# Group tables first, two recurrences summed on TensorE, the gate in the denominator, corrections in opposite row halves, and new orders

## The chip, the cores and the metric

The kernel runs on one core of a Trainium2 chip. The metric is the device time of one execution in microseconds (us). TensorE is called PE in the profile, its weight loads PEld; VectorE is DVE, ScalarE is ACT, GpSimd is POOL, and SyncE (SP) only issues DMAs.

## The reference, cut to what matters

`x` and `f` are 4 batches of 256 tokens by 256 channels. A bidirectional recurrence is computed for every batch and used as a token mixer twice (layer 1 ahead of the attention with gate `r = x`, layer 2 ahead of the feed-forward part with the new `x`):

```python
nf, df = scan(ekv, ek)            # a = a*decay + ekv ; b = b*decay + ek, forward in time
nb, db = scan(ekv, ek, reverse)   # the same backward
num = nf + nb - ekv + euk*vf
den = df + db - ek + euk
out = sigmoid(r) * (num / maximum(den, 1e-8)) * (0.8 + 0.2*tf)
```

Then come 16 query heads over 4 key heads with normed queries and keys, causal softmax and `Wo`; `x` is added. Then a router takes the 8 best of 64 experts in 8 groups, with a softmax inside each group (`soft`), and a gated feed-forward of 8 groups of 176 columns follows:

```python
xg = x[:, None, :] + einsum('ngi,ghi->ngh', soft, mask_up_w)
g, u = xg @ gate_proj, xg @ up_proj      # per group
y = sum over groups of scalar * (silu(g) * u) @ down_proj
```

The kernel never forms `xg`. It multiplies `mask_up_w` with the gate and up tables once (the group tables), and adds `soft @ table` as one extra matmul, the correction, to `x @ gate_proj` and to `x @ up_proj`.

## The kernel before, in words

Everything stays in SBUF with channels or tokens on the 128 partitions. Products that need accuracy are made of three fp32r matmuls (high by high, high by low, low by high; the helper `three`); small ones are single fp32 matmuls, each of which is two instructions in the profile.

Each engine runs a written list of steps in order. `START` holds the first steps of each engine by hand. Then `make_plan` walks through places 0 to 38; in each place the engine's entry in `ORDERS` says in which order it takes the parts of 32 attention items (A is a query projection, B its transposes, C scores, X exp, S the softmax sums, D transposes of the probabilities, E values, F the `Wo` product of two items), the key and value steps (`kv`) and the background steps (`bg`: weight splits, recurrence calls, routing). After place 38 the feed-forward part runs over 22 tiles of 128 columns (11 for each half of the tokens): GA is the gate product of a tile, GB the up product, Y the down product of the tile two back.

Start. SP loads `fT`, the constants, `xT`, the key weights and the eight group tables (six into buffers that are free early, two through the staging buffers). DVE computes the recurrence of batch 0, `("wkv", 1, 0, k)`: k=2 the product (L878), k=3 and 4 the four scans (L868) and the bonus term (L888), k=5 and 6 the sums and the division by way of ACT's Ln and Exp (L893 to L917). Then ACT rounds the result to `RH` (L693), DVE forms the rest `RL` (L921), and PE begins with the key projection K1. The table products `("R", g)` (L1171, eight matmul instructions for each group in fp32) stand behind the first K1. Batch 1 follows on DVE in the same manner. Table results wait in the PSUM banks `acc` and are copied by ACT (L747) and DVE (L1038) into `EX`. The gate of layer 1 is ACT's tanh of `xT` (L666) and a multiply by `1 + tanh` on the numerator (L909).

Feed-forward. PE order is GA, GB, Y for every tile. GA and GB are six matmuls of 128x512 each (L1126 to L1128) and then the correction `EX` by `SX` over all 128 rows (L1303; two of them in tile 5 of each half, which touches both halves of the table). `SX` is made by two transposes in `route` (L1268), a copy (L804) and a DVE step (L1000). DVE then forms the product (L1099, L1103, L1108), ACT and POOL split it (L822, L616), and Y follows.

Of the kernel before, what the change touches and what calls it, by code (L numbers as in the profile page):

```python
# [17 lines left out]
E = G * GS  # L18
# [15 lines left out]
def table_col(g):  # L34

    return g * FI - SECOND * (g // 4)
EXP_CAP = math.exp(KCAP)

# [13 lines left out]
            ("rest", 0)],  # L52
    "DVE": [("kv", 0), ("kv", 0), ("bg", 0), ("kv", 0), ("bg", 0), ("A", 0), ("D1", 4),
            ("kv", 0), ("bg", 0), ("F", 6), ("N", 0), ("S", 2), ("rest", 0), ("kv", 0),
            ("L", 5), ("C", 1)],
    "POOL": [("bg", 0), ("S", 2), ("bg", 0), ("bg", 0), ("rest", 0)],
# [3 lines left out]
    "ACT": ["GT", "split", "last", "GH"],  # L60
# [17 lines left out]
def kv_k(p, half):  # L78
# [5 lines left out]
    "PE": [("split", "K", 0), ("small",), ("split", "Q", 0), ("K1", 0, 0), ("R", 0), ("K1", 0, 1), ("R", 1),  # L84
           ("R", 2), ("R", 3), ("R", 4), ("R", 5), ("K3", 0, 0), ("K3", 0, 1)],
    "ACT": [("wkv", 1, 0, 1), ("tanh", 0), ("tanh", 1), ("tanh", 2), ("tanh", 3), ("logs",), ("wkv", 1, 0, 6),
            ("split", "K", 0), ("wkv", 1, 0, 7), ("small",), ("wkv", 1, 1, 1), ("split", "Q", 0), ("K1", 0, 0), ("K1", 0, 1),
            ("K2", 0, 0), ("wkv", 1, 1, 6), ("K3", 0, 0), ("K3", 0, 1)],
    "DVE": [("wkv", 1, 0, 0), ("wkv", 1, 0, 2), ("wkv", 1, 0, 3), ("wkv", 1, 0, 4), ("wkv", 1, 0, 5), ("wkv", 1, 0, 6), ("wkv", 1, 0, 8),
            ("wkv", 1, 1, 0), ("split", "K", 0), ("wkv", 1, 1, 2), ("wkv", 1, 1, 3), ("wkv", 1, 1, 4), ("K1", 0, 0), ("K1", 0, 1),  # L90
            ("wkv", 1, 1, 5), ("K2", 0, 0), ("wkv", 1, 1, 6)],
    "POOL": [("split", "K", 0), ("small",)],
# [3 lines left out]
    "PE": {"R": None, "split": None, "small": None, "K1": None, "V": None, "K3": None, "GA": None, "GB": None,  # L96
           "route": (0, 1, 3, 4, 6, 7, 8)},
    "ACT": {"split": None, "small": None, "K1": None, "V": None, "K2": None, "K3": None, "table": None,
            "wkv": (1, 6, 7), "gate": (0, 1), "route": (0, 2, 3, 5, 6, 7, 8)},
    "DVE": {"K1": None, "K2": None, "table": None, "onehot": None, "wkv": (0, 2, 3, 4, 5, 6, 8), "gate": (0, 1),  # L100
            "route": (1, 2, 4, 5, 6, 7)},
    "POOL": {"split": None, "small": None, "zeros": None},
# [13 lines left out]
def make_plan(engine, order, ffn_order):  # L116
# [7 lines left out]

    for i, st in ((2, ("split", "V", 0)), (0, ("R", 6)), (0, ("R", 7)), (0, ("table", 0)), (3, ("table", 1)),
                  (2, ("onehot",)), (15, ("zeros",)),
                  (10, ("split", "K", 1)), (17, ("split", "V", 1))):
        put(bg, i, st)
    calls = {(1, 1): [0, 0, 0, 0, 0, 0, 0, 0, 0], (1, 2): [3, 4, 4, 4, 4, 6, 6, 7, 7], (1, 3): [7, 8, 8, 8, 10, 11, 12, 12, 12],
             (2, 0): [12, 13, 13, 14, 14, 15, 16], (2, 1): [18, 19, 19, 19, 20, 21, 21],  # L130
             (2, 2): [21, 21, 22, 22, 23, 24, 24], (2, 3): [25, 26, 26, 26, 26, 28, 28]}
# [7 lines left out]
    for n, back in enumerate([-2, -2, -2, -1, -3, -2, -2, -3]):  # L139
        put(bg, max(first_tile(*divmod(n, NKV)) + back, 0), ("split", "Q", n))  # L140
    for n, on in enumerate([5, 5, 5, 5, 3, 5, 5, 4]):
        put(bg, first_tile(*divmod(n, NKV)) + on, ("split", "O", n))
    early = [31, 35, 37]
# [3 lines left out]
    for half, places in (((0, 1), [2, 4, 4, 5, 5]), ((1, 0), [15, 15, 15, 16, 17]), ((1, 1), [17, 18, 18, 19, 19])):  # L147
        for i, st in zip(places, kv_k(*half)):
            put(kv, i, st)
    for p, places in ((0, [3, 5, 6, 6]), (1, [21, 21, 23, 24])):  # L150
        for t, i in enumerate(places):
            put(kv, i, ("V", p, t))
    ahead = []
    for f, places in enumerate(([36, 37, 37], [45, 45, 45])):
# [39 lines left out]
    for st, f in zip(last, [0, 1, 2, 3, 4, 5, 6, 6, 8, 9, 10]):  # L194
        if concerns(engine, st):
            per[f].append(st)
# [23 lines left out]
BLOCKS = [s for s in PLAN if s[0] in ("small", "split") or s[0] == "R" and s[1] >= 6]  # L220
# [3 lines left out]
BLOCK_COLS = {"R": 4 * FI, "small": 256, "K": 1024, "V": 1024, "Q": 1024, "O": 1024, "F": 768}  # L224
# [39 lines left out]
ND = {1: 17, 2: 16}  # L264
NA = {1: 5, 2: 4}


def wkv_before(count, layer, b):

    return sum(count[call[0]] for call in WKV_CALLS[:WKV_CALL[(layer, b)]])  # L270


def last_call(layer, b):
    return wkv_before(ND, layer, b) + ND[layer]
# [40 lines left out]

def spread_count(f):
# [4 lines left out]
def program(nc, ins, out, group_scalars):  # L321
    ctx = ExitStack()
    with ctx:
# [21 lines left out]
        half = sb("half", [P, B])  # L345
        half_mix = sb("half_mix", [P, B])
        edec = sb("edec", [P, 8])
# [9 lines left out]
        E2, F2, B2 = (sb(n, [P, 2 * CH * TE]) for n in ("E2", "F2", "B2"))  # L357
# [11 lines left out]
        V = sb("V", [P, TPP, NKV * D])  # L369
# [15 lines left out]
        bmask = V[:, :, :].rearrange("p t n -> p (t n)").rearrange("p (c g d e) -> p c g d e", c=CH, g=G, d=16)  # L385
        mup = sb("mup", [P, CH, E])

        def early_table(g):

            if g < 4:  # L390
# [24 lines left out]

        acc = [pb("acc0"), pb("acc1")]
# [6 lines left out]
        names = """consts_in vecs_in cond_in side_in0 side_in1 side_in2 side_in3 x_in0 x_in1 x_in2 x_in3 table_in0 table_in1 table_in2 table_in3 table_in4 table_in5 mup_in imap_in stores_done  # L423
        pads_ready half_ready init_act init_dve zeros_ready key_scale_ready bmask_ready onehot_ready scalars_out
        split_hi split_lo ffn_used
        wkv_act wkv_dve tanh1_done r1_ready r2_ready tanh2_done base_gated rh2_done
# [56 lines left out]
        def _(sp):  # L483
            def load(n):
                step = BLOCKS[n]
                if n >= NSTAGE:
                    old = BLOCKS[n - NSTAGE]
                    if old[0] == "R":
                        sp.wait_ge(s["table_full"], RNO[old] + 1)
                    else:  # L490
                        sp.wait_ge(s["split_lo"], SPLIT_NO[old] + 1)
                w = BLOCK_COLS[step[1] if step[0] == "split" else step[0]]
                if step[0] == "R":
                    src = ins["tables"][step[1]]
                elif step[0] == "small":
# [17 lines left out]
            side(0)  # L513
            sp.dma_start(const[:], ins["const"]).then_inc(s["consts_in"], 16)
            main(0)
            sp.dma_start(mup[:], ins["mup"]).then_inc(s["mup_in"], 16)
            main(1)
            main(2)
            main(3)
            load(0)  # L520
            side(1)
            table(0)
            table(1)
            table(2)
            load(1)
            table(3)
            load(2)
            table(4)
            table(5)
# [5 lines left out]
            def spread_scalars(f):  # L535
                p, m = divmod(f, FT)
                if m == 0:
                    tok = slice(p * PT_, (p + 1) * PT_)
                    sp.wait_ge(s["rt_act"], 7 * p + 7)
# [22 lines left out]
        def _(pool):  # L562
# [7 lines left out]
            linked(pool.memset(V[:], 0.0))  # L570
# [3 lines left out]
            pool.wait_ge(s["mup_in"], 16)  # L574
            for g in range(G):
# [796 lines left out]
```

## Time and profile before

| | before |
|---|---|
| median of 3 runs | 420.47 us (418.64 to 420.99) |
| the profiled execution: its time / its span | 419.07 us / 417.3 us |
| PE busy | 367.4 us (88%) |
| DVE busy | 331.4 us (79%) |
| ACT busy | 275.9 us (66%) |
| POOL busy | 218.5 us (52%) |
| chain that ended last | PE 53%, DVE 25%, ACT 15%, issue 5% |

The span goes from the first to the last instruction; the time of the execution has 1.8 us more around it. Busy shares are means over the span: PE does next to nothing in the first 20 us and is never idle in the feed-forward part, so the table is to be read together with the rows by stretch.

### The profile page before, as it was taken

Reading aid. Unit: us, or ns where it says so; the run is one execution under the profiler, and the core shown is the slowest. Engines: PE = TensorE matmul, PEld = TensorE weight load, DVE = VectorE, ACT = ScalarE, POOL = GpSimd, SP = SyncE. Lnnn points to the kernel's source line nnn. Section 1 sums busy time; section 2 is a strip of 40 time slices with the busy share of each in tenths; the row PEclk is TensorE's granted clock in tenths of the full one; section 3 lists DMA queues with packets and bytes.
Section 4 is the critical chain, followed back from the end, with each engine's and each line's share of the span. In section 5 each row is a group of like instructions: output and inputs, shape, how many; then the busy total and the mean of one; then the engine's idle time right before and its main releaser. Section 6 shows DMA issues by size and latency. Waiting matters only on the chain.

```text
span 417.3 us, 6425 instructions
## 1 busy us (share of the span) xinstructions
PE 367.4 (88%) x1952; PEld 294.3 (71%) x1952; DVE 331.4 (79%) x779; ACT 275.9 (66%) x673; POOL 218.5 (52%) x229
## 2 busy tenths in 40 slices
PE   0098778899999789898998987999899999999995
PEld 0097566688878667687776876687587878888884
DVE  8999788999988997789999889486557777665543
ACT  5547778798889498696976887785375434453321
POOL 7160613179524858225585121464259756888831
PEclk9999989999999999999999999999999999999999
DMA  7735300113100304001031000111065343274121
GB/s 214 297 87 183 104 0 0 52 52 102 53 0 2 102 0 137 15 3 50 2 101 40 1 2 0 38 41 38 2 160 172 138 126 81 97 218 173 53 75 50
DMA packets 14209, 31.92 MB, mean 76 GB/s; under 512 B 1872, under 2 KB 4432, under 8 KB 14176
## 3 DMA queue, kind: packets, MB, share of 16 engines
q1 hardware_dynamic: 13888, 31.38, 23.6%
q8 instruction: 16, 0.26, 0.3%
q10 hardware_dynamic: 288, 0.14, 0.1%
q14 instruction: 17, 0.14, 0.1%
HBM read 30.43 MB, written 1.08 MB: 76 GB/s over the span
## 4 chain that ended last, share of the span: by engine, by line
PE 53%; DVE 25%; ACT 15%; issue 5%; POOLq 0%; POOL 0%; DVEq 0%; ACTq 0%
PE ov L1223 6%; PE sc L1201 5%; PE acc L1126 4%; PE acc L1127 4%; PE acc L1128 4%; PE tr L1152 4%; ACT PR L623 4%; DVE B L868 3%; DVE F L868 3%; DVE PR L1062 3%; PE proj L1140 3%; PE tr L1128 2%; PE tr L1126 2%; PE tr L1127 2%; PE sc L1126 2%
## 5 line engine op out<-in xcount | busy, mean ns | idle before, releaser
L596 POOL TENSOR_TENSOR WL<-stage,WH 128x256 fp32r<-128x256 f32 x142 | 125.9, 916 | 75.1 <-ACT WH L662 75.1
L610 POOL TENSOR_TENSOR PR<-PR,RI 128x512 f32<-128x512 f32 x48 | 53.6, 1133 | 83.8 <-DVE RI L1072 83.8
L1140 PE MATMUL proj<-WH,RH 128*128 128x512 f32 x96 | 42.5, 443 | 33.0 <-DVE RL L921 19.9
L1126 PE MATMUL acc<-OH,WH 128*128 128x256 f32 (+1 forms) x172 | 54.5, 317 | 2.9 <-DVE OL L1084 2.2
L623 ACT ACTIVATE PR<-PR,MX 128x128 f32<-128x128 f32 (+1 forms) x128 | 56.9, 458 | 0.0
L1127 PE MATMUL acc<-OL,WH 128*128 128x256 f32 (+1 forms) x172 | 53.1, 309 | 0.0
L1128 PE MATMUL acc<-OH,WL 128*128 128x256 f32 (+1 forms) x172 | 53.0, 308 | 0.0
L1201 PEld LDWEIGHTS sc<-kT,QT 128*128 128x128 f32 x256 | 41.6, 193 | 16.1 <-issue 12.9
L1201 PE MATMUL sc<-kT,QT 128*128 128x128 f32 (+1 forms) x256 | 47.8, 330 | 0.0
L1223 PE MATMUL ov<-PTS,V 128*128 128x512 f32 x96 | 46.6, 594 | 1.1 <-DVE OL L1084 1.1
L1140 PEld LDWEIGHTS proj<-WH,RH 128*128 128x128 f32 x96 | 18.4, 192 | 39.5 <-issue 37.2
L1062 DVE CUSTOM_DVE_ANT_0 PR<-sc,const,RQ 128x128 f32<-128x128 f32 (+1 forms) x128 | 45.5, 412 | 0.1
L822 ACT CAST OH<-PR 128x512 fp32r<-128x512 f32 x22 | 13.7, 623 | 42.2 <-DVE PR L1108 42.1
L616 POOL TENSOR_TENSOR OL<-PR,OH 128x512 fp32r<-128x512 f32 x22 | 28.9, 1312 | 22.5 <-ACT OH L822 21.0
L662 ACT CAST WH<-stage 128x768 fp32r<-128x768 f32 (+1 forms) x42 | 39.3, 937 | 0.0
L1141 PE MATMUL proj<-WH,RL 128*128 128x512 f32 x96 | 38.7, 403 | 0.0
L1126 PEld LDWEIGHTS acc<-OH,WH 128*128 128x128 f32 x172 | 32.4, 188 | 6.0 <-issue 2.8
L1099 DVE SCALAR_TENSOR_TENSOR PR<-PR,sc 128x512 f32<-128x512 f32 x22 | 15.1, 686 | 25.1 <-ACT PR L814 25.1
L1128 PEld LDWEIGHTS acc<-OH,WL 128*128 128x128 f32 x172 | 32.4, 188 | 2.0
L1127 PEld LDWEIGHTS acc<-OL,WH 128*128 128x128 f32 x172 | 32.4, 188 | 2.0
L927 DVE TENSOR_REDUCE SS<-SQ 128x4 f32<-128x512 f32 x40 | 26.8, 677 | 5.5 <-ACT SQ L719 5.5
L1144 PE MATMUL proj<-WL,RH 128*128 128x512 f32 x96 | 30.8, 402 | 0.0
(160 smaller groups left out, 878.4 us busy)
## 6 DMA issues: line engine op xcount, KB each, us to landing
stage<-in_ffn SPq DMA_DIRECT2D x22, 384.0 KB, 3.3
stage<-in_wq SPq DMA_DIRECT2D x8, 512.0 KB, 3.3
stage<-in_wo SPq DMA_DIRECT2D x8, 512.0 KB, 3.4
SBC<-group_scalars SPq DMA_DIRECT2D x8, 256.0 KB, 3.6
PR<-in_tables SPq DMA_DIRECT2D x4, 352.0 KB, 7.2
fT<-in_fT SPq DMA_DIRECT2D x4, 256.0 KB, 3.8
xT<-in_xT SPq DMA_DIRECT2D x4, 256.0 KB, 4.1
stage<-in_wk SPq DMA_DIRECT2D x2, 512.0 KB, 4.7
```

The lines of the kernel that those rows point to most:

```text
L596: i = pool.tensor_tensor(lo[:, c:c + 256], src[:, c:c + 256], hi[:, c:c + 256].bitcast(F32), ALU.subtract)
L610: pool.tensor_tensor(pr, pr, RI[:, m % 4, hs[0]:hs[0] + nh].rearrange("p (h o) -> p h o", o=1).broadcast_to([P, nh, 512 // nh]), ALU.mult) ...
L623: return nc.scalar.activation(o, i, ACT.Exp, **k)
L662: nc.scalar.copy(WH[:, slot, 0:w], src[:, 0:w]).then_inc(s["split_hi"], 1)
L1062: i = v.tensor_tensor_reduce(PR[:, u % 6, w * k:w * k + w], sc[u % 2][:, w * k:w * k + w], mask[:, 256 - w:256], RQ[:, n % NST, half_, h:h ...
L1126: mm(o, lh, rh, start=first, stop=False, skip_group_check=True)
L1127: mm(o, lh, rl, start=False, stop=False, skip_group_check=True)
L1128: return mm(o, ll, rh, start=False, stop=last, skip_group_check=True)
L1140: mm(proj[:], rh[ch], wh[ch], start=ch == 0, stop=False, skip_group_check=True)
L1141: mm(proj[:], rl[ch], wh[ch], start=False, stop=False, skip_group_check=True)
L1201: i = mm(sc[u % 2][:, w * k:w * k + w], QT[:, m % 3, h, :], kT[:, g, T * bb:T * bb + w], start=True, stop=True)
L1223: i = mm(ov[:], V[:, 2 * bb + c, g * D:(g + 1) * D], PTS[:, m % 2, c, :, :].rearrange("p h n -> p (h n)"), start=(c == 0), stop=(c == ti))
```

## The change

1. **Tables.** All eight table products stand in PE's `START` list, R0 to R6 ahead of the first key projection and R7 right behind it, and all eight tables are loaded early, each into a free buffer. SP's order is new: `fT` of batch 0, `mup`, table 0, the constants, `xT` of batch 0, tables 1 and 2, the key weights, tables 3 and 4, `fT` of batch 1, tables 5 to 7, the router's weights, `xT` of batch 1, the query weights, and only then `xT` of batches 2 and 3. POOL lays out the masked table of `mup` with one copy in place of eight. The rows of the up table are rotated by 64 against those of the gate table (`table_rows`), so each copy of a group is made in two pieces of 176 columns in place of one of 352.
2. **Sums.** For batches 0 and 1 of layer 1 PE adds the forward recurrence, the backward one and the bonus term by identity matmuls in fp32 into PSUM (three for the denominator, three for the numerator). DVE reads the sums there.
3. **Gate.** ACT makes `exp(-x)` in place of tanh, POOL clamps it and adds 1, and DVE multiplies it into the denominator in the step that takes the maximum (all four batches of layer 1). The multiply on the numerator is gone.
4. **Projections** issue the two matmuls that need only `RH` before they wait for `RL`.
5. **Corrections.** A tile's correction reads only the 64 rows of its pair of groups: for the gate product in one row half, for the up product in the other. From tile 2 on, both are issued one after the other ahead of GA's six matmuls, into two PSUM banks. Tiles 2 and 8 of each half still use all 128 rows; tile 5 has the pair and one full correction for each product. Tiles 0 and 1 issue a 64-row correction at the end of GA and of GB. The up corrections need `SX` with its row halves exchanged (`SY`), which two DMAs on SP's queue make for each half of the tokens.
6. **Orders.** `ORDERS`, the places of many background steps and GB of tile 0 are changed.

```diff
     "PE": [("R", 0), ("R", 1), ("R", 2), ("sum", 0, 0), ("R", 3), ("sum", 0, 1), ("sum", 0, 2),
            ("R", 4), ("R", 5), ("R", 6), ("K1", 0, 0), ("R", 7), ("split", "K", 0), ("small",),
            ("split", "Q", 0), ("K1", 0, 1), ("sum", 1, 0), ("sum", 1, 1), ("K3", 0, 0), ("K3", 0, 1), ("sum", 1, 2)],
     "ACT": [("ex", 0), ("wkv", 1, 0, 1), ("wkv", 1, 0, 6), ("ex", 1), ("split", "K", 0), ("wkv", 1, 0, 7), ("small",), ...
...
-    "PE": [("kv", 0), ("kv", 0), ("kv", 0), ("kv", 0), ("kv", 0), ("D0", 4), ("bg", 0),
-           ("A", 0), ("kv", 0), ("D1", 4), ("kv", 0), ("F", 6), ("E", 5), ("bg", 0),
-           ("kv", 0), ("C", 1), ("B", 0), ("rest", 0)],
+    "PE": [("kv", 0), ("kv", 0), ("kv", 0), ("kv", 0), ("bg", 0), ("D0", 4), ("A", 0),
+           ("kv", 0), ("D1", 4), ("kv", 0), ("F", 6), ("E", 5), ("bg", 0), ("kv", 0),
+           ("C", 1), ("B", 0), ("kv", 0), ("bg", 0), ("rest", 0)],
...
+                elif st[0] == "sum":
+                    _, b, k = st
+                    n0 = wkv_before(ND, 1, b)
+                    for x, n, kind in ((DF, 3, 0), (DB, 4, 0), (EUX[:], 5, 0), (NF, 6, 1), (NB, 7, 1), (EU[:], 9, 2)):
+                        if kind == k:
+                            pe.wait_ge(s["wkv_dve"], n0 + n)
+                            i = mm(sum_bank(b, min(k, 1)), ident, x, start=n in (3, 6), stop=n in (5, 9), skip_group_check=True)
...
                 elif k == 5:
+                    if summed(L, b):
+                        dve.wait_ge(s["sum_ready"], 2 * b + 1)
+                        dve.wait_ge(s["gate_ready"], b + 1)
+                        done(v.scalar_tensor_tensor(out=DF, in0=sum_bank(b, 0), scalar=1e-8, in1=gate1(b), op0=ALU.max, op1=ALU.mult))
+                        return
...
+                elif st[0] == "ex":
+                    b = st[1]
+                    act.wait_ge(s[f"x_in{b}"], 16)
+                    exp(gate1(b), xT[:, :, cols(b)], scale=-1.0).then_inc(s["gate_exp"], 1)
...
+                    def both(h, row, first, last):
+                        i = correct(0, h, slice(row, row + 64), first, last)
+                        correct(1, h, slice(64 - row, 128 - row), first, False)
+                        return i
...
+                    side_by_side = f >= 2 and pairs
+                    if side_by_side and a == 0:
+                        wait_bank(1)
+                        wait_soft(1)
+                        both(*pairs[0], True, False)
...
+                    for r in (0, 64):
+                        sp.dma_start(turned_soft(p)[64 - r:128 - r, :, :].bitcast(F32), SX[r:r + 64, :, tok].bitcast(F32)).then_inc(s["soft_turned"], 16)
```

## Rows read from the trace of the kernel before

**Rows 1.** The page, busy time of the engines over the span.
```profile
PE 367.4 (88%) x1952; PEld 294.3 (71%) x1952; DVE 331.4 (79%) x779; ACT 275.9 (66%) x673; POOL 218.5 (52%) x229
```
**Rows 2.** Busy time by stretch: stretch, length, busy of each engine, clock, DMA share, GB/s.
```profile
21.00:45.00 24.00, 20.99 (x117) 18.62 (x115) 22.89 (x39) 15.04 (x32) 10.44 (x9) 1.00 0.39 119
45.00:80.00 35.00, 28.65 (x137) 22.18 (x138) 29.04 (x85) 27.68 (x76) 11.75 (x14) 0.95 0.14 45
200.00:300.00 100.00, 92.11 (x538) 72.31 (x537) 82.61 (x239) 74.15 (x199) 43.91 (x46) 1.00 0.09 27
340.00:360.00 20.00, 20.00 (x95) 16.07 (x94) 16.25 (x23) 9.24 (x16) 14.58 (x16) 1.00 0.29 82
```
**Rows 3.** Waits of PE: for whom, us in total, times, longest.
```profile
PE proj L1140 <- DVE RL L921: 19.9, 1, 19.9
```
**Rows 4.** Timeline of batch 0: start, length, engine, line, operation.
```profile
9.69 1.20 DVE L868 TENSOR_TENSOR_SCAN B<-DEC,E 128x514 f32<-128x514 f32 x1
13.67 0.43 DVE L899 TENSOR_SCALAR F<-F 128x512 f32<-128x512 f32 x1
17.59 0.75 DVE L917 SCALAR_TENSOR_TENSOR F<-F,half_mix 128x512 f32<-128x512 f32 x1
18.38 0.62 ACT L693 CAST RH<-F 128x512 fp32r<-128x512 f32 x1 [2.02 <-DVE F L917]
```
**Rows 5.** Timeline of batch 1 on DVE.
```profile
30.78 0.69 DVE L895 TENSOR_TENSOR EU<-EUX,fT 128x512 f32<-128x512 f32 x1
31.39 0.69 DVE L897 TENSOR_TENSOR F<-F,EUX 128x512 f32<-128x512 f32 x1
37.83 0.75 DVE L917 SCALAR_TENSOR_TENSOR F<-F,half_mix 128x512 f32<-128x512 f32 x1
38.50 2.35 DVE L1038 SCALAR_TENSOR_TENSOR EX<-EX,const,acc 32x352 fp32r<-32x352 f32 x4
```
**Rows 6.** Timeline of PE: two matmuls of the first projection, then table products.
```profile
20.43 0.63 PE L1141 MATMUL proj<-WH,RL 128*128 128x512 f32 x1
20.86 0.63 PE L1140 MATMUL proj<-WH,RH 128*128 128x512 f32 x1
22.57 2.29 PE L1171 MATMUL acc<-PR,V 128*128 128x176 f32 x8
29.66 2.55 PE L1171 MATMUL acc<-PTS,V 128*128 128x176 f32 x16
```
**Rows 7.** The chain that ended last: two fp32 value matmuls of 512 columns.
```profile
79.19 1.72 PE ov L1223 x4
```
**Rows 8.** Timeline: POOL's mask copies in the first 12 us.
```profile
6.02 5.70 POOL L576 COPY V<-mup 128x48 f32<-128x48 f32 x8 [2.00 <-DMA mup<-in_mup]
```
**Rows 9.** The page's DMA issues: count, KB of each, median us from issue to landing.
```profile
SBC<-group_scalars SPq DMA_DIRECT2D x8, 256.0 KB, 3.6
```
**Rows 10.** The page, DMA traffic in 40 slices of 10.4 us.
```profile
GB/s 214 297 87 183 104 0 0 52 52 102 53 0 2 102 0 137 15 3 50 2 101 40 1 2 0 38 41 38 2 160 172 138 126 81 97 218 173 53 75 50
```
**Rows 11.** Timeline of PE around four 64-row transposes inside the feed-forward part.
```profile
321.63 0.40 PE L1128 MATMUL acc<-OH,WL 128*128 128x512 f32 x1
321.95 0.32 PEld L1255 LDWEIGHTS proj<-const,LT 64*128 64x128 f32 x4 [0.37 <-issue]
321.96 0.46 PE L1255 MATMUL proj<-const,LT 64*128 64x64 f32 x4
322.35 0.19 PEld L1126 LDWEIGHTS sc<-RH,WH 128*128 128x128 f32 x1
...
322.69 0.39 PE L1127 MATMUL sc<-RL,WH 128*128 128x512 f32 x1
...
322.92 0.40 PE L1128 MATMUL sc<-RH,WL 128*128 128x512 f32 x1
```
**Rows 12.** Timeline: `SX` of the first half complete, and GB's first correction.
```profile
301.30 0.75 DVE L1000 SCALAR_TENSOR_TENSOR SX<-SX,const,proj 128x512 fp32r<-128x512 f32 x1 [1.97 <-ACT SX L804]
...
306.98 0.39 PE L1303 MATMUL tr<-SX,EX 128*128 128x512 f32 x1
```

More of the change, by code:

```diff
@@ L59 @@
     "PE": ["GA", "GB", "Y", "last", "split"],
-    "ACT": ["GT", "split", "last", "GH"],
+    "ACT": ["GT", "last", "split", "GH"],
     "DVE": ["GU", "last", "out"],
@@ L83 @@
 START = {
[L84 to L92, printed above, removed]
[3 rows of a table added]
+    "ACT": [("ex", 0), ("wkv", 1, 0, 1), ("wkv", 1, 0, 6), ("ex", 1), ("split", "K", 0), ("wkv", 1, 0, 7), ("small",),
+            ("wkv", 1, 1, 1), ("split", "Q", 0), ("K1", 0, 0), ("K1", 0, 1), ("K2", 0, 0), ("wkv", 1, 1, 6), ("K3", 0, 0),
+            ("K3", 0, 1)],
@@ L101 @@
             "route": (1, 2, 4, 5, 6, 7)},
-    "POOL": {"split": None, "small": None, "zeros": None},
+    "POOL": {"ex": None, "split": None, "small": None, "zeros": None},
 }
@@ L218 @@
 PLAN = PLANS["PE"]
-BLOCKS = [s for s in PLAN if s[0] in ("small", "split") or s[0] == "R" and s[1] >= 6]
+BLOCKS = [s for s in PLAN if s[0] in ("small", "split")]
 BLOCK_NO = {s: n for n, s in enumerate(BLOCKS)}
@@ L313, in group_rows, with table_rows, packed @@
     return [(g, max(g * FI - P * m, 0), min((g + 1) * FI - P * m, P)) for g in range(first, last + 1)]
+def table_rows(g, a):
+    first = 32 * ((g + 2 * a) % 4)
+    return slice(first, first + 32)
+def packed(m):
+    pairs = sorted({g // 2 for g, _, _ in group_rows(m)})
+    return [] if len(pairs) == 2 and pairs[0] // 2 == pairs[1] // 2 else [(q // 2, 64 * (q % 2)) for q in pairs]
 def spread_count(f):
@@ L513, in _ @@
             side(0)
+            sp.dma_start(mup[:], ins["mup"]).then_inc(s["mup_in"], 16)
+            table(0)
             sp.dma_start(const[:], ins["const"]).then_inc(s["consts_in"], 16)
             main(0)
-            sp.dma_start(mup[:], ins["mup"]).then_inc(s["mup_in"], 16)
+            table(1)
+            table(2)
+            load(0)
+            table(3)
+            table(4)
+            side(1)
+            table(5)
+            table(6)
+            table(7)
+            load(1)
             main(1)
+            load(2)
             main(2)
             main(3)
[L520 to L529, printed above, removed]
             sp.dma_start(imap[:], ins["imap"]).then_inc(s["imap_in"], 16)
@@ L1296, in _ @@
                     for ch in range(CH):
                         w = wblock(wst, 256 * a + P * ch, 256 * a + P * ch + P)
-                        three(bank[:], w[0], w[1], RH[:, p, ch, :], RL[:, p, ch, :], ch == 0, False)
-                    pe.wait_ge(s["rt_vec"], 6 * p + 6)
-                    if f == 0:
-                        pe.wait_ge(s["table_lo"], 2)
-                    for h, c0 in halves:
-                        i = mm(bank[:], EX[:, h, a, c0:c0 + P], SX[:, h, tok], start=False, stop=(h, c0) == halves[-1], skip_group_check=True)
+                        i = three(banks[a][:], w[0], w[1], RH[:, p, ch, :], RL[:, p, ch, :], ch == 0 and not side_by_side,
+                                  bool(side_by_side) and ch == CH - 1 and len(pairs) == 1)
@@ new lines, in _ @@
+                    if side_by_side and len(pairs) == 2:
+                        i = correct(a, pairs[1][0], slice(0, P), False, True)
+                    if not side_by_side:
+                        wait_soft(a)
+                        if pairs:
+                            h, row = pairs[0]
+                            row = 64 - row if a else row
+                            i = correct(a, h, slice(row, row + 64), False, True)
+                        else:
+                            i = correct(a, group_rows(m)[0][0] // 4, slice(0, P), False, True)
```

241 lines of the change are left out of this document (146 added, 95 removed), and 9 rows, old and new, of tables (ORDERS, START).

## The prediction, as put on record

> **What bounds the kernel now.** I read the busy shares first [rows 1]: PE is busy for 367.4 of 417.3 us, DVE for 331.4, so neither alone explains the span. The busy time by stretch [rows 2] says where each counts. From 340 to 360 us, as in the whole feed-forward part from about 303 on, PE is busy 20.00 of 20.00 us: whatever PE does more or less there moves the end one for one. From 21 to 45 DVE is busy 22.89 of 24.00 and PE 20.99, but much of that PE work is table products that nobody waits for. From 45 to 80 PE idles 6.4 us, from 200 to 300 7.9 us. Then the waits of PE: one of 19.9 us [rows 3], for the first projected batch. So there are three parts: a start that runs at DVE's pace, a middle in which PE is the bound with small holes, and an end that is PE alone.
>
> **The start, batch 0.** Before, its scans end at 9.69 + 1.20 = 10.89, its result (L917) at 18.34 and the rounded copy at 19.00 [rows 4]. After, the bonus step moves between the scans, so the four scans end at about 11.5. PE must first do R0 to R2, then three fp32 identity matmuls. R0 waits for the mask: POOL's eight copies take 5.70 us [rows 8]; one copy of the same 384 columns is shown nowhere, between 0.7 (one of eight) and 5.7; I take 1.1, and `mup` is issued two DMAs sooner, so R0 starts near 6.3. A group costs 2.29 us at the slow matmul pace and half of 2.55, 1.27, at the fast one [rows 6]; that these are the two levels 1.2 and 2.4 GHz is read from the pace, 0.43 us from one 512-column matmul to the next at 20.43 and 20.86 [rows 6] against 0.23 later [rows 11]. PE began at 19.9, its table products from 22.57 still run at the slow pace, and everything from 24.6 on is fast. If it rises as soon after R0, R0 is slow, R1 mixed, R2 fast: 6.3 + 2.3 + 2.1 + 1.3 = 12.0. An fp32 matmul of 512 columns costs 1.72 / 2 = 0.86 us at the fast level [rows 7], three 2.6: the denominator stands at 14.6, about 0.5 later than the 14.10 at which the maximum step ends now [rows 4]. The numerator's three (2.6) and R3 (1.3) follow, until 18.5, and DVE's last step ends at 19.3 where it ended at 18.34.
>
> Between this and the key projection stands one new wait. ACT's `exp` for batch 1 is queued ahead of the key weights' cast and of batch 0's rounded copy, and waits for `xT` of batch 1, which SP now issues sixteenth. By the sizes listed 4.98 MB come before its end. The first two slices moved 2.23 and 3.10 MB [rows 10], which puts it at 10.4 + 2.75/0.297 = 19.7; with the tables, whose packets are larger, moved into the first slice, it can be 16.5. I take 18: exp to 18.6, cast to 19.65, copy to 20.3. DVE leaves batch 0 about 1.0 us later than now. K1 then finds PE free only after R4 to R6 (3.8 us), near 22.3, and ends near 23.7 at the fast pace, where it ends at 22.8 now; DVE reads it much later, so this is hidden behind the scans of batch 1.
>
> **Batch 1.** Between its scans and its result DVE loses two sums of the denominator, two of the numerator and the gate multiply, at 0.61 us apart (30.78 to 31.39, [rows 5]) 3.05 us, and gets 0.2 back, since the maximum step of 0.43 [rows 4] becomes one of 0.69: 2.85 saved. PE's six identity matmuls for it, 5.2 us, fall between 24 and 36, where 6.2 us and more of table products are gone: no cost. Result of batch 1: 38.58 now [rows 5], less 2.85, plus 1.0. The copies of tables in two pieces: DVE's four take 2.35 us [rows 5]; eight of half the columns cost between the same and double, I take +0.5. Start in sum: +1.0 - 2.85 + 0.5 = **-1.4** (bounds -3.5 and +2.5).
>
> **The middle.** Batches 2 and 3 lose the gate multiply and keep the adds: 2 x (0.61 - 0.2) = -0.8, worth that much where DVE leads. The granted clock was 0.95 of full from 45 to 80 [rows 2], after holes in PE's work: 5% of 35, 1.7 us, is lost to the 1.2 GHz level; if PE gets its first items earlier and with fewer holes, part comes back: -1.0 (bounds 0 and -1.7). The new orders cannot be priced from rows: they can at best close the holes of rows 2, of which I count less than half (-6), and can open new ones (+4); I take **-1.5**. The early matmuls on `RH` alone save nothing in the middle, where `RL` is long ready. Middle: **-3.3**.
>
> **The feed-forward part, where I look hardest.** Now a correction is one 128-row matmul at 0.23 us (322.69 to 322.92, [rows 11]); a pair 0.46. Of 22 tiles, tiles 2 and 8 of each half stay as they are and tiles 0 and 1 of the first half are single: 16 pairs. The trace has no 64-row pair, but it has 64-row matmuls amid 128-row ones. The last 128-row one starts at 321.63 and would give way at 321.86. The 64-row weights are not loaded ahead, as all others are: the load starts at 321.95. The next 128-row load starts at 322.35, also not ahead, and its matmul streams from 322.69 - 0.23 = 322.46, which prices a bare load at 0.11. In all 0.60 us for four loads that take 0.32 together: at least **0.28 us of switching** per visit [rows 11]. The other three visits of this kind look the same. A pair then costs 0.28 + load 0.11 + second load under the first matmul 0.11 + one stream 0.21 = 0.71, 0.25 more than now: 16 x 0.25 = 4.0. The four single ones cost 0.28 + 0.11 + 0.21 = 0.60 against 0.23: 4 x 0.37 = 1.5. Sum **+5.5**; bounds: if the two halves don't overlap, 16 x 0.11 more, +7.3; if nothing is switched, -3.7. I take +5.5, since it is the nearest row.
>
> The Trainium skill, TensorEngine Tiling (Array Packing), Key Properties, says that changing the tiling mode drains the array, though tiles within a mode work in parallel. The trace agrees with the drain, 0.09 us before the load and the missing prefetch; by its promise of up to 2x alone, the term would be -3.7.
>
> Waits added there: GB of tile 0 needs `SX` turned. `SX` is whole at 302.05 [rows 12], two issues on SP and a landing of 3.6 us (the scalars' loads of like size, [rows 9]) give 306.4, ahead of 306.98 where its first correction stands; behind PE is everything, so each us of lateness would count. GA of a tile now also waits for the up bank of the tile two back, free before in all but the routing stretches. SP's two DMAs a half lie ahead of the group scalars, for which DVE has waited already, and are hidden by PE's backlog. All at 0, bound +1.5.
>
> **Sum.** -1.4 - 3.3 + 5.5 = +0.8 on the profiled execution's 419.07 us (span 417.3 and 1.8 around it): 419.9. That execution lies 1.4 below the median of 420.47, by which it would be 421.3. I predict **420.5**.
>
> **Rivals.** (1) The likeliest, as above: start and middle give about what the end takes. Chance 0.50; own range 416.5 to 425.
>
> (2) The row halves work side by side with no switching cost. Each pair costs one matmul: -3.7 in place of +5.5, 9.2 less, 411 to 412. For it: fp32r streams of 512 columns appear nowhere in the visits I measured, those were fp32 of 64. Against it: all visits show the gap. Chance 0.30. The Trainium skill, TensorE: Matmul & The Clock Gate, Part 3, reports four 32-row tiles of 512 columns at 3.07 times; no row here shows one.
>
> (3) Slower: PE is not yet at 2.4 GHz when the sums come. R0 to R2 at 2.29 each from 6.3 reach 13.2, and three sums at the slow pace take 5.2, so the denominator comes at 18.4 in place of 14.6; DVE stands behind it, and all of batch 1. Start +3.8: 424.3. It decides from a rise later than about 12 us. Chance 0.12.
>
> (4) The orders open holes: the middle is +4 in place of -1.5, 426. Chance 0.08.
>
> A measurement of this kernel tells 0.5%, 2.1 us. Case 1 gives faster 0.10, same 0.22, slower 0.18; case 2 0.29 and 0.01; case 3 same 0.02, slower 0.10; case 4 same 0.02, slower 0.06. Faster 0.39, same 0.27, slower 0.34. Cases of both signs hold the chance, so the range reaches from case 2 to case 4: 411 to 427.
>
> **What would show it.** The first K1 matmul at 22 to 23; the result of batch 1 near 36.7; GA's pair at 0.7 us from the matmul before it to the first full one after (0.25 to 0.35 if I am wrong); the feed-forward part from its first GA to the end longer by 5 us. Denominator sums later than 16 us speak for case 3. The prediction fails above all if the 64-row visit is cheap for fp32r, or if the holes in the middle close by more than I count.

## The result, and the profile after

The changed kernel takes 428.50 us in the median (426.87 to 428.93, 4 runs) where the kernel before takes 419.62 (418.64 to 420.99, 4 runs): ratio 1.0208, 95% interval 1.0175 to 1.0240. It is 8.9 us slower, above my range of 411 to 427.

The page of the profiled execution (busy times, the clock by slices):

```profile
PE 386.0 (90%) x1976; PEld 297.6 (70%) x1976; DVE 331.8 (78%) x776; ACT 276.1 (65%) x680; POOL 216.3 (51%) x226
...
PEclk9998989899999999999999999999999999999999
```

The windows of [rows 2], with the same columns:

```profile
21.00:45.00 24.00, 20.09 (x84) 13.28 (x83) 21.77 (x33) 15.68 (x33) 9.07 (x9) 0.93 0.28 88
45.00:80.00 35.00, 25.74 (x124) 19.99 (x123) 28.89 (x91) 28.66 (x82) 13.93 (x15) 0.95 0.09 31
200.00:300.00 100.00, 94.83 (x567) 76.22 (x565) 85.58 (x246) 78.15 (x211) 40.41 (x43) 1.00 0.09 27
340.00:360.00 20.00, 20.00 (x93) 15.48 (x92) 16.65 (x25) 7.70 (x14) 14.60 (x16) 1.00 0.36 103
```

PE is busy 18.6 us longer in a span 9.3 us longer; part of it is new work, the twelve identity matmuls at 0.86 us each, and part is the same work at half the clock. From 45 to 80 it is busy for 25.74 us, with 9.3 us of holes where there were 6.4: what the reordering was hoped to close has opened. From 21 to 45 the granted clock is 0.93 where it was 1.00.

The start, by the timeline (compare [rows 4] and [rows 5]):

```profile
6.82 6.35 PE L1246 MATMUL acc<-PR,VX 128*128 128x176 f32 x24 [6.82 <-DMA const<-in_const]
10.32 1.23 DVE L921 TENSOR_TENSOR_SCAN F<-DEC,E 128x514 f32<-128x514 f32 x1
14.73 1.02 PE L1255 MATMUL sc<-EUX,const 128*128 128x512 f32 x2
15.79 0.69 DVE L965 SCALAR_TENSOR_TENSOR F<-sc,TH 128x512 f32<-128x512 f32 x1 [0.28 <-PE sc L1255]
19.56 0.76 DVE L938 SCALAR_TENSOR_TENSOR F<-ov,full_mix,F 128x512 f32<-128x512 f32 x1 [0.30 <-PE ov L1255]
20.35 0.62 ACT L742 CAST RH<-F 128x512 fp32r<-128x512 f32 x1 [0.90 <-DVE F L938]
22.82 0.75 PE L1218 MATMUL proj<-WH,RH 128*128 128x512 f32 x2
37.54 0.75 DVE L938 SCALAR_TENSOR_TENSOR F<-ov,full_mix,F 128x512 f32<-128x512 f32 x1 [0.74 <-PE ov L1255]
38.67 3.25 DVE L1115 SCALAR_TENSOR_TENSOR EX<-EX,const,acc 32x176 fp32r<-32x176 f32 x8 [0.38 <-ACT EX L799]
```

DVE waits twice for sums of PE. The result of batch 0 ends at 20.32 (18.34 before), that of batch 1 at 38.29 (38.58 before), and the copies of the first half of the table take DVE 3.25 us instead of 2.35. In between, the scans of batch 1 begin at 23.34 where they began at 21.71.

What follows on PE is the first query projection and the first scores. In the kernel before:

```profile
33.79 1.26 PE L1152 MATMUL tr<-const,RT 128*128 128x128 f32 x8 [1.58 <-DVE RT L1027]
34.89 1.36 PE L1171 MATMUL acc<-stage,V 128*128 128x176 f32 x8
...
37.01 0.62 PE L1144 MATMUL proj<-WL,RH 128*128 128x512 f32 x2
...
36.00:39.00 3.00, 3.00 (x20) 2.73 (x19) 2.93 (x5) 2.77 (x7) 0.00 (x0) 1.00 0.53 172
```

In the changed kernel:

```profile
34.33 1.26 PE L1232 MATMUL tr<-const,RT 128*128 128x128 f32 x8 [2.06 <-DVE RT L1103]
...
36.52 1.84 PE L1218 MATMUL proj<-WH,RH 128*128 128x512 f32 x2
38.16 1.05 PE L1221 MATMUL proj<-WH,RL 128*128 128x512 f32 x2
...
36.00:39.00 3.00, 3.00 (x6) 1.65 (x5) 1.85 (x4) 2.56 (x9) 0.00 (x0) 0.50 0.01 3
```

The table products that filled PE here are gone, it idles 2.06 us ahead of the key transposes (1.58 before), and from 36 to 39 us the granted clock is 0.50, the 1.2 GHz level. The first scores start at 42.39, where they started at 40.48: 1.9 us are lost before the second half of the table is copied.

Then the waits of PE from 40 to 100 us (total, times, longest):

```profile
PE proj L1218 <- ACT VX L791: 3.4, 3, 2.7
PE sc L1287 <- DVE MX L1139: 2.9, 1, 2.9
PE proj L1218 <- ACT SQ L768: 2.8, 2, 1.5
```

The middle one is new: scores wait for the maxima of the scores before them, which DVE has behind the copies of the second half of the table. The experiments turn on it. The first one has grown: its longest wait is 2.7 us, ahead of 80.06, where the kernel before has one of 1.0.

The feed-forward part, PE timeline around a pair of 64-row corrections (the column behind the tiles is rows by columns of the array in use):

```profile
354.35 0.60 PE L1356 MATMUL proj<-const,ST 128*128 128x128 f32 x4
354.88 0.49 PE L1392 MATMUL sc<-SX,EX 64*128 64x512 f32 x1
354.88 0.49 PE L1392 MATMUL tr<-SY,EX 64*128 64x512 f32 x1
355.30 0.50 PE L1203 MATMUL sc<-RH,WH 128*128 128x512 f32 x1
355.64 0.40 PE L1204 MATMUL sc<-RL,WH 128*128 128x512 f32 x1
```

The two start together. A 0.40 us record holds the 0.23 us from one full matmul to the next and 0.16 of pipeline, so the stream before ends at 354.79 and the first full stream behind begins at 355.64 - 0.23 = 355.41: the visit takes 0.62 us.

Milestones: PE's first `Wo` product starts at 91.2 us (85.1 before), its first product of the feed-forward part at 304.68 (300.34), its last at 422.57 (413.32). So 4.3 us have been lost by 304.7, and the feed-forward part is 117.9 long, not 113.0: 4.9 more. At 91 us 6.1 were lost; 1.8 of them are won back by 304.7.

### The profile page after: what moved, and what is told of

Read it like the earlier page. It is cut to its first block, busy times and chain, and to the rows that moved or that the text cites. A ratio compares the mean times of both kernels' runs of the same rounds, so it can differ in the third digit from the quotient of the medians.

```text
span 426.6 us, 6520 instructions
## 1 busy us (share of the span) xinstructions
PE 386.0 (90%) x1976; PEld 297.6 (70%) x1976; DVE 331.8 (78%) x776; ACT 276.1 (65%) x680; POOL 216.3 (51%) x226
## 4 chain that ended last, share of the span: by engine, by line
PE 56%; DVE 22%; ACT 14%; issue 5%; DMA 2%; SPq 1%; POOLq 0%; POOL 0%; ACTq 0%; DVEq 0%
PE ov L1311 6%; PE sc L1287 5%; PE tr L1232 5%; PE acc L1203 4%; PE acc L1205 4%; PE acc L1204 4%; DVE B L921 3%; DVE PR L1139 3%; PE sc L1203 3%; DVE F L921 3%; PE proj L1218 3%; ACT PR L674 2%; PE proj L1221 2%; PE tr L1203 2%; PE sc L1204 2%
## 5 line engine op out<-in xcount | busy, mean ns | idle before, releaser
L643 POOL TENSOR_TENSOR WL<-stage,WH 128x256 fp32r<-128x256 f32 x142 | 120.9, 880 | 94.2 <-ACT WH L713 94.2
L661 POOL TENSOR_TENSOR PR<-PR,RI 128x512 f32<-128x512 f32 x48 | 52.7, 1115 | 77.2 <-DVE RI L1149 77.2
L1311 PE MATMUL ov<-PTS,VX 128*128 128x512 f32 x96 | 46.6, 594 | 1.1 <-DVE OL L1161 1.1
L1218 PE MATMUL proj<-WH,RH 128*128 128x512 f32 x96 | 36.0, 457 | 11.9 <-ACT SQ L768 5.8
L667 POOL TENSOR_TENSOR OL<-PR,OH 128x512 fp32r<-128x512 f32 x22 | 29.2, 1328 | 14.6 <-ACT OH L874 13.5
L1232 PE MATMUL tr<-const,PR 128*128 128x128 f32 x192 | 29.2, 277 | 4.2 <-ACT QT L806 1.6
L1221 PE MATMUL proj<-WH,RL 128*128 128x512 f32 x96 | 30.9, 404 | 0.0
L1232 PEld LDWEIGHTS tr<-const,PR 128*128 128x128 f32 x192 | 22.8, 142 | 10.9 <-issue 6.4
```

What stands on the lines that cost most here:

```text
L643: i = pool.tensor_tensor(lo[:, c:c + 256], src[:, c:c + 256], hi[:, c:c + 256].bitcast(F32), ALU.subtract)
L661: pool.tensor_tensor(pr, pr, RI[:, m % 4, hs[0]:hs[0] + nh].rearrange("p (h o) -> p h o", o=1).broadcast_to([P, nh, 512 // nh]), ALU.mult) ...
L1218: mm(proj[:], rh[ch], wh[ch], start=ch == 0, stop=False, skip_group_check=True)
L1221: mm(proj[:], rl[ch], wh[ch], start=False, stop=False, skip_group_check=True)
L1232: i = tp(tr[t % 2][:, P * k:P * k + P], x, ident)
L1311: i = mm(ov[:], V[:, 2 * bb + c, g * D:(g + 1) * D], PTS[:, m % 2, c, :, :].rearrange("p h n -> p (h n)"), start=(c == 0), stop=(c == ti))
```

## The experiments

Ratios are to the kernel before, with 95% intervals; us that are worked out from ratios are shares of 419.6.

### 1. Key weights' exponential ahead of the first gate exponential

```diff
-    "ACT": [("ex", 0), ("wkv", 1, 0, 1), ("wkv", 1, 0, 6), ...
+    "ACT": [("wkv", 1, 0, 1), ("ex", 0), ("wkv", 1, 0, 6), ...
```

In the changed kernel ACT's list begins with a step that waits for `xT` of batch 0 until 8.34 us; the scans start at 10.32.

> ACT's first gate exponential, which waits for xT of batch 0 until 8.34 us, is issued behind the exponential of the keys instead of ahead of it. Theory A (that wait is what delays the start and all behind it): the scans of batch 0 begin near 6.5 us instead of 10.3, its result comes 2 to 4 us sooner than 20.3, and the kernel gets 3 to 4 us faster than the changed one (about 425). Theory B (PE's first three table groups, until 13.0 us, and the sums queued behind them set batch 0): the scans move but the denominator still leaves PE at 15.6, the result stays at 20.3 within 0.5 us, and the time stays at 428.5 within 1.

Measured 428.45 us, 1.0221 (1.0205 to 1.0237): nothing gained. The scans began at 7.81, 2.5 us sooner, and the step that makes the result of batch 0 began at 20.67, 1.1 us later than before the edit (19.56). DVE waited 3.40 us for PE's sum of the denominator: PE, with tables and sums, sets it.

### 2. Corrections and table layout as before

The changed kernel with whole 128-row corrections, no rotation, no `SY`, and table copies in one piece; starts, sums, gate and orders stay.

```diff
-    first = 32 * ((g + 2 * a) % 4)
+    first = 32 * (g % 4)
...
-                        both(*pairs[0], True, False)
...
+                    for h, c0 in halves:
+                        i = mm(bank[:], EX[:, h, a, c0:c0 + P], SX[:, h, tok],
```

> The corrections, the table copies and the row layout go back to those of the kernel before (all 128 rows, at the end of GA and GB, no exchanged halves, copies in one piece); all else is as changed. Theory A (the visits of PE to 64-row form cost what was forecast): the stretch from GB of tile 0 to the end shrinks by 4 to 5 us, and table copies give about 1 to 2 us more: 422 to 424. Theory B (the loss in the feed-forward part comes from the new waits and DMAs or from the orders): at most 1 to 2 us faster than the changed kernel.

Measured 421.17 us, 1.0051 (1.0035 to 1.0066). Of the 8.9 us this takes 6.6 back by the ratios, more than the corrections can owe; about half comes ahead of the feed-forward part (first `Wo` product at 88.0 us, not 91.2; first product of the feed-forward part at 301.44, not 304.68). The feed-forward part is 114.07 us long, still 1.1 more than in the kernel before. Runs 6, 9, 13, 14 and 15 follow the half ahead of it.

### 3. Both together

Edits 1 and 2.

> Both of the edits above. If they are independent, the gains add: 419 to 421 if the first exponential matters by itself, 422 to 424 if it does not.

Measured 420.46 us, 1.0033 (1.0021 to 1.0045): 0.8 us below run 2 by the ratios, the intervals overlap. It is the base of runs 7, 8, 11 and 12.

### 4. Each 64-row correction alone

```diff
-                    side_by_side = f >= 2 and pairs
+                    side_by_side = False
```

> The changed kernel with no two corrections side by side: each tile issues its 64-row correction at the end of GA and again at the end of GB, so 32 visits where there were 16. Theory A (the cost is one of each visit, near 0.4 us above a full correction): 16 x (2 x 0.61 - 0.62) = 9.6 us slower than the changed kernel, near 438. Theory B (the visit costs little, the wait ahead of GA costs): no slower, or faster by 1 to 2 us.

Measured 437.29 us, 1.0431 (1.0410 to 1.0452), 9.4 us above the changed kernel by the ratios. 32 visits in place of 16: what is paid is paid for each visit.

### 5. Both corrections in the same row half

```diff
-                        correct(1, h, slice(64 - row, 128 - row), first, False)
+                        correct(1, h, slice(row, row + 64), first, False)
```

> The changed kernel, but the up correction of each pair reads the same 64 rows as the gate correction, so the two cannot be in opposite halves (its values are then those of other groups; the number and form of the instructions are unchanged). Theory A (opposite halves do run at the same time): each of the 16 pairs grows from 0.62 to about 0.83 us, one stream of 0.21, so 3.4 us slower than the changed kernel, near 432. Theory B (they never overlapped, the pair's cost was two streams all along): no difference, 428.5.

Measured 431.57 us, 1.0294 (1.0263 to 1.0326), 3.6 us above. The timeline of PE around a pair:

```profile
354.50 0.60 PE L1356 MATMUL proj<-const,ST 128*128 128x128 f32 x4
355.03 0.49 PE L1392 MATMUL sc<-SX,EX 64*128 64x512 f32 x1
355.37 0.39 PE L1392 MATMUL tr<-SY,EX 64*128 64x512 f32 x1
355.68 0.50 PE L1203 MATMUL sc<-RH,WH 128*128 128x512 f32 x1
356.02 0.40 PE L1204 MATMUL sc<-RL,WH 128*128 128x512 f32 x1
```

The second starts 0.34 behind the first, not with it: opposite halves do run side by side, for about 0.22 us a pair (3.6 / 16).

### 6. Pieces without rotation

Run 2 with each group's copy in two pieces of 176 columns.

> The kernel with whole-row corrections (the run that took 421.17), but its table copies are made in two pieces of 176 columns on ACT and DVE, as in the changed kernel. Theory A (the pieces, which stand in front of the first scores on DVE, are what costs 3.3 us ahead of the feed-forward part): 3 us slower than that run, near 424. Theory B (the row layout or the mask costs): within 0.5 us of 421.2.

Measured 421.09 us, 1.0052 (1.0035 to 1.0069), as run 2. Pieces alone cost nothing here. The copies of one half of the table took 2.01 us on ACT and 2.88 on DVE, against 2.43 and 3.25 in the changed kernel, for as many pieces of the same size.

### 7. Only batch 1 summed on TensorE

```diff
-    return layer == 1 and b < SUMMED
+    return layer == 1 and b == 1
```

On run 3; batch 0 is added on DVE again.

> The kernel with whole-row corrections and the exponential of the keys first (420.46), but PE sums batch 1 only; batch 0 is summed on DVE as before. Theory A (PE's tables and sums are the gate of batch 0): its result comes near 18 us instead of 19.7 to 20.3, and the time falls by 1 to 2 us to about 419. Theory B (a lead of batch 0 is used up by batch 1's own order on DVE and PE): within 0.5 us of 420.5.

Measured 420.34 us, 1.0019 (1.0002 to 1.0036), no different from run 3. Batch 0 again ended at 20.2. DVE had met another hindrance near its start:

```profile
5.06 1.73 DVE L895 TENSOR_SCALAR half<-tf 128x4 f32<-128x4 f32 x1
```

The same step of 4 columns takes 0.17 us in run 11.

### 8. Orders of before on the new start

Run 3 with `ORDERS` and the places of the background steps as they were.

> The kernel with whole-row corrections and the exponential of the keys first (420.46), with the orders and places of the kernel before; the hand-written starts stay. Theory A (the new orders bring the 1.5 us that were forecast): 1 to 2 us slower, 421.5 to 422.5. Theory B (the new orders fit the old costs no better): the same within 0.5 us, or faster.

Measured 425.97 us, 1.0164 (1.0134 to 1.0193): 5.5 us slower than run 3. PE has no wait for the maxima from 40 to 100 us, as in the kernel before; other waits are longer, such as one of 2.3 us ahead of a query projection (1.3 in run 3).

### 9. Rotation without 64-row corrections

Run 6 with the up table's rows rotated and `SY` made, but all corrections over 128 rows.

```diff
-    first = 32 * (g % 4)
+    first = 32 * ((g + 2 * a) % 4)
...
+                        i = mm(bank[:], EX[:, h, a, c0:c0 + P], turned_soft(p)[:, h, :] if a else SX[:, h, tok],
```

> The kernel with whole-row corrections and table copies in pieces (421.09), plus the rotated rows of the up table and the two DMAs that exchange the halves of SX; the corrections still read all 128 rows at the end of GA and GB. Theory A (the rotated layout, whose copies change rows with every instruction, costs the 3 to 4 us that the changed kernel loses ahead of the feed-forward part): 424 to 425, with GB of tile 0 starting near 310. Theory B (that loss belongs to the 64-row form alone or is drift of the schedule): 421 within 0.7, at most 1 more for the DMAs.

Measured 425.58 us, 1.0150 (1.0129 to 1.0171): 4.1 us above run 6 by the ratios. Copies (2.43 and 3.25), the wait for the maxima (2.9) and the first `Wo` product (91.6) are as in the changed kernel.

### 10. The kernel before with the new orders

> The kernel before with only the new orders and places; its starts, sums, gate and corrections stay. Theory A (the new orders are better by themselves, as their 5.5 us in the run with the old orders suggest): 3 to 5 us faster than the kernel before, near 415. Theory B (orders fit only the costs that they were made for, so old with old and new with new): same as the kernel before or 1 to 4 us slower.

Measured 417.94 us, 0.9969 (0.9956 to 0.9981): 1.3 us faster than the kernel before, and the fastest kernel of the study. Its feed-forward part begins 2.3 us sooner (298.04) and is 1.1 us longer (114.10), so 1.1 us of what the new orders take from the middle comes back at the end. The wait for the maxima is there, too, with 1.10 us:

```profile
52.20 1.13 PE L1201 MATMUL sc<-kT,QT 128*128 128x128 f32 x8 [1.10 <-DVE MX L1062]
```

Against run 2, which has the same orders, the same corrections and the new start, sums and gate, it is 3.4 us faster by the ratios. Its first scores start at 40.49 (42.90 in run 2), and its clock from 21 to 45 us is 1.00 (0.93).

### 11. POOL clears the table ahead of the mask copy

Run 7, with POOL's clearing of `EX` moved ahead of its wait for `mup`.

> The kernel that sums batch 1 only on PE (420.34), with POOL's clearing of the table buffer ahead of the mask copy, as before. In that kernel DVE's small step beside the clearing took 1.73 us in place of 0.17 and the product 1.29 in place of 0.69. Theory A (POOL and DVE hold each other up there, and the start is DVE's): the scans begin near 6.4 in place of 7.8 and the time falls by 1 to 1.5 us. Theory B (absorbed at PE or later): within 0.4 us of 420.3.

Measured 420.06 us, 1.0017 (1.0001 to 1.0034), as run 7. DVE ended batch 0 at 18.5, 1.8 us sooner, but `RL` waited 1.39 us for ACT's `RH`, and the lead was gone.

### 12. No sums on TensorE

Run 7 without the sums of batch 1.

> The kernel that sums batch 1 only (420.34), with no sums on PE at all. Theory A (the sums of batch 1 shorten DVE's chain by 2.9 us at no cost, as forecast): 2 to 3 us slower, near 423. Theory B (PE's 5.2 us and the wait for its last sum eat the gain): within 0.7 us.

Measured 421.82 us, 1.0065 (1.0048 to 1.0082), 1.9 us above run 7 by the ratios: that is what the sums of batch 1 are worth. The result of batch 1 came at 40.13, 2.5 us later than in run 7 (37.58). PE, which had the sums to do in run 7, idled 9.1 us ahead of the key transposes and had a clock of 0.79 from 21 to 45 us (0.93), so part of the 1.9 can be the clock's.

### 13. Rotated, copies in an order that keeps the rows

```diff
-                    for g in range(4 * h, 4 * h + 4):
+                    for r in range(4):
                         for a in range(2):
+                            g = 4 * h + (r + 2 * a) % 4
                             rows = table_rows(g, a)
```

On run 9; the same eight pieces, and the two on the same rows follow each other.

> The rotated up table with whole-row corrections as in the run before it that measured 425.58 us, but the eight copies of a table half are ordered so that the two pieces that lie on the same 32 rows follow each other: the rows change four times in place of eight. Theory A (what the rotation costs comes from the change of rows between one small copy and the next, 46 to 50 ns each on ACT and DVE, 0.8 us for both engines and each half of the table): half of it goes, copies take 2.2 and 3.1 us in place of 2.43 and 3.25, and the time falls by at least 1.5 us, to 423 to 424. Theory B (the rotation costs in some other way, in the table products or by the exchanged copy of the softmax): the copies get shorter and the time stays at 425 to 426.

Measured 422.32 us, 1.0067 (1.0041 to 1.0093), 3.5 us below run 9 by the ratios. I had miscounted: rows change seven times in the old order and three times in the new one, which is the count of run 6, too. The copies take what they took there, 2.01 and 2.88. Each of four changes had cost 0.105 us on ACT (0.42 / 4) and 0.09 on DVE (0.37 / 4).

### 14. The same order in the changed kernel

> The changed kernel whole, with the copies of a table half in the same new order and nothing else. Theory A: 426 to 427 us, about 2 less than the 428.5 of the changed kernel. Theory B: 428 to 429.

Measured 425.77 us, 1.0140 (1.0115 to 1.0166): 2.9 us below the changed kernel by the ratios, with no instruction more or less.

### 15. Longer copies without rotation

Run 6 with every gate piece cut in two again, twelve copies in place of eight for each half of the table.

> No rotation, whole-row corrections, copies in pieces, as in the run that measured 421.09 us, but the gate piece of every group is cut in two once more: twelve copies for each half of the table in place of eight. By the step from four to eight (ACT 1.79 to 2.01 us, DVE 2.35 to 2.88) this adds 0.2 us on ACT and 0.5 on DVE for each half, together as much as the rotation added. Theory A (what counts is only how long ACT and DVE are held, whatever makes them longer): 423 to 425 us. Theory B (the rotation costs in another way than by the time of the copies): 421 to 421.5.

Measured 424.22 us, 1.0115 (1.0091 to 1.0138): 2.6 us above run 6, with 2.22 and 3.40 us of copies. The second scores and the windows from 45 to 60 us (PE busy, PEld, DVE, ACT, POOL, granted clock, DMA) show why so little weighs so much. Run 6:

```profile
54.08 1.13 PE L1283 MATMUL sc<-kT,QT 128*128 128x128 f32 x8 [1.75 <-DVE MX L1135]
...
45.00:60.00 15.00, 10.42 (x54) 8.07 (x53) 12.66 (x52) 12.74 (x43) 7.79 (x9) 1.00 0.20 70
```

Run 15:

```profile
55.82 2.05 PE L1283 MATMUL sc<-kT,QT 128*128 128x128 f32 x8 [2.72 <-DVE MX L1135]
...
45.00:60.00 15.00, 11.02 (x49) 9.09 (x48) 12.88 (x53) 11.52 (x42) 8.23 (x11) 0.89 0.20 70
```

The changed kernel:

```profile
56.07 1.98 PE L1287 MATMUL sc<-kT,QT 128*128 128x128 f32 x8 [2.92 <-DVE MX L1139]
...
45.00:60.00 15.00, 10.55 (x46) 8.62 (x46) 12.74 (x48) 11.67 (x38) 7.39 (x9) 0.89 0.21 70
```

And run 14, which differs from it by the order of the copies alone:

```profile
54.45 1.13 PE L1289 MATMUL sc<-kT,QT 128*128 128x128 f32 x8 [1.73 <-DVE MX L1141]
...
45.00:60.00 15.00, 10.66 (x54) 8.24 (x53) 12.77 (x51) 12.61 (x42) 8.17 (x9) 1.00 0.21 70
```

Where PE had idled 1.7 us ahead of these scores (runs 6, 13, 14; 1.1 in run 2), it stayed at 2.4 GHz and the eight matmuls took 1.13. Where it had idled 2.7 to 2.9 in the changed kernel and in runs 9 and 15, part of the stretch was granted at 1.2 GHz and they took 1.6 to 2.05. But it does not always go so: runs 1, 4 and 5 have the same wait of 2.93 us and took 1.13 for the eight, with 0.93 granted from 45 to 60 us in runs 1 and 4, and 1.00 in run 5. A clock of 0.89 over 15 us is up to 1.65 us lost; with 1.2 us more of waiting that is 2.8, the size of what runs 14 (2.9) and 15 (2.6) measured.

For run 14 this sum leaves something out. Its query projection behind those scores starts at 58.68, 3.2 us sooner than in the changed kernel (61.91). But from 60 to 80 us its own clock is 0.90 (1.00 in the changed kernel), the lead at the first `Wo` product is 2.1 us, and it is 2.5 at the end of the profiled executions. That row changes cost 2.9 us here and 3.5 in run 9 is shown by the times (runs 14 and 13). How much of that is waiting and how much is clock is argued, from one profiled execution of each kernel.

## Why the prediction was wrong

**The feed-forward part: the mechanism was right, the size too high.** +5.5 was forecast for its visits. The part is 4.9 us longer, but that number agrees partly by luck. By the lengths of the part: 113.0 before, 114.1 with the new orders alone (run 10) as with run 2, 114.8 with rotation and `SY` (run 13), 117.7 with the 64-row visits, too (run 14). So the visits account for 3.0; the times of runs 14 and 13 say the same, 0.73% or 3.1 us, uncertain by 1.5. One by one, a pair takes 0.62 us (forecast 0.71), since both weight loads start together instead of one under the other's matmul, and the period of a plain tile is 4.79 us where it is 4.63 in run 13. A single takes 0.61 (forecast 0.60). By these sizes the visits would be worth 16 x 0.16 + 4 x 0.38 = 4.1; why the part grows by 1.1 less stays open. The wait for `SY`, counted at 0 with a bound of 1.5, is 0.8 us, and it stands in the second half of the tokens (366.25), where I had called the exchange hidden. Rival 2 falls: halves do overlap (run 5), but they save 0.2 a pair and the visit costs more (run 4). The Trainium skill, TensorEngine Tiling (Array Packing), Key Properties, states both the drain and the parallel tiles, and the trace agrees with both, at 0.62 us for the pair against 0.46 for two full matmuls.

**The step that failed is the start with the middle**: -1.4 and -3.3 forecast, +4.3 measured where the feed-forward part begins. By its terms:

- *Copies of the tables, "+0.5"*: this is the largest. I priced their durations between one and two times, and the durations were not far off (DVE +0.9 in place of +0.5 for the first half), but I took them for a cost that ends with itself. I left out two things: that changing rows from piece to piece has a price of its own, and that the same copies come a second time, from 47.7 to 53.4 us, with ACT and DVE both ahead of the maxima that PE's scores wait for. Row changes alone cost 2.9 us in the changed kernel (run 14), 3.5 in run 9 against run 13.
- *Clock, "-1.0"*: nothing came back. From 45 to 80 us it is 0.95 as before, from 21 to 45 it is 0.93 and from 80 to 92 it is 0.86, both 1.00 before: up to 1.7 us lost in each of the two. I had written that PE's six sums fill the place of the table products at no cost; by the rows shown above, PE idled longer ahead of the key transposes and ran the first query projection at 1.2 GHz.
- *Batch 0, "+1.0"*: +2.0. PE waited for the constants until 6.82, where I had let it wait for the mask until 6.3 (POOL's one copy took 0.59 us, under my bound of 0.7), and three table products took 6.35 us, not 5.7; so the denominator's sum ended at 15.75 rather than at 14.6. I had put PE on the path, rightly; I had missed that ACT's list begins with a wait for `xT`, which did no harm of its own (run 1). DVE instead of PE for these sums gave the same time (run 7), and so did a batch 0 that ended 1.8 us sooner on DVE (run 11), with ACT's copy behind it.
- *Batch 1, "-2.85"*: run 12 puts the sums at 1.9 us of time, and at 2.5 us of batch 1's result. But the scans began 1.6 us later, and DVE waited 0.74 for the numerator, so the result came at 38.29, not at 36.7.
- *Orders, "-1.5"*: right in sign both times; they give 1.3 us on the kernel before (run 10) and 5.5 on the new start (run 8), inside my bound of -6. Rival 4 falls. The orders do bring one hole, the wait of 1.1 us for the maxima (run 10), but they close more; the row changes lengthen just this one. Whether row changes would cost anything in the old orders, where that wait is not seen, was not run.

Put together by the ratios: row changes 2.9 us (changed kernel against run 14), 64-row visits 3.1 (14 against 13), rotation and `SY` besides 0.7, which is within the uncertainty (13 against 2), and 2.1 for start, sums, gate and orders (run 2), which is 3.4 for start, sums and gate (2 against 10) less 1.3 for the orders. The sum must come out at the 8.7 us measured, since each step starts where the other ends; it shares the loss out and does not test it. Rival 3 falls: the sums began at 13.01, close to the 13.2 that it has, but ran at the fast pace, 0.86 us from one to the next (13.87 to 14.73 by the timeline), and the denominator came at 15.75, under the 16 that I had named for that case.

Left open: what in the start makes up its 3.4 us. The traces show where it lies. The first scores of run 2 start 2.4 us later than those of run 10, and between the key transposes and these scores 1.35 us of it arise, where run 2 has the clock of 0.59 from 36 to 39 us and run 10 has 1.00. That the missing table products brought this about is argued from the rows, not tested. Runs 1, 4 and 5 kept 1.00 in that window, but came 1.1 to 1.5 us later to the key transposes, so that their first scores start no sooner than in the changed kernel. Runs 1, 3, 7 and 11 each took one suspect away and gained at most 0.8 us. I did not undo alone the eight table products ahead of the first key projection, the gate in the denominator, or SP's new order. Of the clock the runs show only what PE did before the stretches that fell to 1.2 GHz and before those that didn't, not why.

## What to carry to other kernels

A small step that runs twice is to be priced at both places, and at each one the question is what PE waits for behind it: 0.8 us of copies for each half of the table became 2.9, with a longer wait and, in the profiled execution, a stretch at 1.2 GHz behind it. Work that is moved ahead is missing where it was: it may have kept PE busy there. Copies to different rows should be ordered so that the rows change seldom. A 64-row matmul amid 128-row ones pays by the visit, so it must replace more than two full matmuls of 512 columns before it gains; and new orders should be timed on the old kernel, where here they won 1.3 us by themselves.

## What the runs showed of the hardware

- Copies of 32 rows by 176 columns from PSUM to SBUF cost 0.1 us more on ACT, and 0.09 on DVE, when they are on other rows than the copy before (runs 9 and 13, same pieces in another order).
- Two 64-row matmuls in opposite row halves have their weight loads side by side as well: 354.87 and 354.88 us, by the timeline of the changed kernel. A pair took 0.62 us between full matmuls, in one half 0.85 (run 5: the stream before ends at 354.94, the full one begins at 355.79), a single one 0.61. The second of an opposite pair is free.
- A step of 4 columns on DVE took 1.73 us in run 7 and 0.17 in run 11, where POOL did not clear its table beside it. In run 7 it began at 5.06, during POOL's mask copy (4.92 to 5.42), and ended at 6.79, as POOL's clearing did (5.36 to 6.77). The two runs differ by the order of these two POOL steps alone; which of the two holds DVE was not isolated.
- In the changed kernel PE ran at 1.2 GHz for a while behind waits of 2.06 us (granted clock 0.50 from 36 to 39 us) and of 2.68 us (0.86 from 80 to 92 us). Runs 1, 4 and 5 had the first of these waits, too, and 1.00 from 36 to 39. Behind a wait of 2.93 us their second scores took 1.13 us, and 1.98 in the changed kernel behind 2.92. So the same wait was followed by either level.
